# Interaction tower with table look-ups: inner pair products in two 64-column tiles, R of the first group filled by ScalarE, and small tables looked up for groups 1 and 2 only

## What is computed

```python
e  = stack([tbl_f[ids[:, f]] for f in range(26)], axis=1)            # 512 x 26 x 32
x1 = einsum('bik,bjk,hij->bhk', e,  e, W1) + b1[None, :, None]       # 128 maps
x2 = einsum('bik,bjk,hij->bhk', x1, e, W2) + b2[None, :, None]
z  = sum(concatenate([x1, x2], axis=1), axis=-1)                     # 512 x 256
h  = relu(concatenate([z, dense_ctx], axis=1) @ W_top1 + b_top1)
h  = relu(h @ W_top2 + b_top2)
y  = h @ W_top3
```

## Time and profile before

| | us |
|---|---|
| median of 3 runs (lowest, highest) | 170.41 (170.31, 170.66) |
| the profiled execution, device time | 170.0 |
| its span, first to last instruction | 168.1 |
| TensorE matmuls busy | 137.4 (82%) |
| VectorE busy | 111.0 (66%) |
| GpSimd busy | 94.9 (56%) |
| ScalarE busy | 65.5 (39%) |

### The profile page before, as it was taken

How to read it: one execution, slowest core, us unless ns; L and a number is a source line. 1 busy time by engine, 2 the same in 40 slices (tenths; PEclk the granted TensorE clock), 3 DMA queues, 4 the chain that set the end, 5 groups by cost and what they waited for, 6 DMA issues and landing times.

```text
span 168.1 us, 3668 instructions
## 1 busy us (share of the span) xinstructions
PE 137.4 (82%) x1414; PEld 124.0 (74%) x1414; DVE 111.0 (66%) x425; ACT 65.5 (39%) x177; POOL 94.9 (56%) x100
## 2 busy tenths in 40 slices
PE   6418999200099979898899999899999979999995
PEld 6305666100099959788898899789899969999993
DVE  7899368999999919999804599980659996000000
ACT  1122888400025870350453730155281024574042
POOL 4778777787778777777777777777760000000000
PEclk9965999955559999999999999999999999999999
DMA  6994331000000312001011331010042000022000
GB/s 129 387 289 157 120 98 23 12 12 13 12 18 8 65 27 75 16 12 16 12 16 17 64 78 25 16 16 12 16 80 59 5 0 4 0 51 65 17 0 0
DMA packets 8537, 8.56 MB, mean 51 GB/s; under 512 B 3128, under 2 KB 7650, under 8 KB 8340
## 3 DMA queue, kind: packets, MB, share of 16 engines
q1 hardware_dynamic: 2668, 4.70, 8.8%
q10 hardware_dynamic: 2908, 2.12, 5.7%
q0 software_dynamic: 2944, 1.51, 5.3%
HBM read 7.28 MB, written 1.04 MB: 50 GB/s over the span
## 4 chain that ended last, share of the span: by engine, by line
PE 60%; DVE 16%; POOL 8%; ACT 6%; DMA 4%; issue 4%; ACTq 0%; DVEq 0%; SPq 0%
PE ring L619 15%; PE z2p L655 14%; POOL emb L317 8%; PE z2p L660 7%; PE ring L625 5%; PE h2y L711 4%; PE ring L639 4%; DVE l L507 3%; DMA emb<-in_tbl,idx 3%; DVE r L499 3%; DVE emb L478 3%; PE ring L648 2%; PE h1p L702 2%; ACT v_in L791 2%; DVE ctx_x L474 2%
## 5 line engine op out<-in xcount | busy, mean ns | idle before, releaser
L317 POOL DMA_INDIRECT emb<-in_tbl,idx x92 | 94.0, 1022 | 29.4 <-issue 27.7
L619 PE MATMUL ring<-r,l 128*128 128x104 f32 x256 | 32.7, 287 | 15.2 <-DVE l L507 15.2
L619 PEld LDWEIGHTS ring<-r,l 128*128 128x128 f32 x256 | 31.9, 203 | 16.3 <-DVE l L507 15.4
L803 ACT COPY t_in<-ring 128x416 f32<-128x416 f32 x32 | 16.2, 506 | 34.2 <-PE ring L619 34.2
L655 PE MATMUL z2p<-t_in,v_in 128*128 128x128 f32 x208 | 24.4, 277 | 0.8 <-ACT v_in L791 0.8
L655 PEld LDWEIGHTS z2p<-t_in,v_in 128*128 128x128 f32 x208 | 23.6, 192 | 1.2 <-ACT v_in L791 1.0
L590 PE MATMUL ring<-w1s,w2t 128*128 128x352 f32 x52 | 17.2, 494 | 4.0 <-DVE w1s L371 4.0
L590 PEld LDWEIGHTS ring<-w1s,w2t 128*128 128x128 f32 x52 | 10.6, 206 | 10.1 <-DVE w1s L371 4.1
L507 DVE TENSOR_TENSOR l<-sg_b,l 128x192 f32<-128x192 f32 (+5 forms) x72 | 15.6, 300 | 0.0
L507 DVE TENSOR_TENSOR l<-sg_a,l 128x192 f32<-128x192 f32 (+5 forms) x72 | 15.6, 298 | 0.0
L474 DVE TENSOR_TENSOR ctx_x<-ring,mask 128x512 f32<-128x512 f32 x6 | 4.1, 691 | 17.2 <-PE ring L639 17.1
(11 more groups left out here) (129 smaller groups left out, 183.3 us busy)
## 6 DMA issues: line engine op xcount, KB each, us to landing
w2t<-in_L_rec_W SPq DMA_DIRECT2D x1, 1664.0 KB, 7.2
emb<-in_tbl,idx POOLq DMA_INDIRECT x92, 2.4
wt<-in_W_top SPq DMA_DIRECT2D x2, 512.0 KB, 8.4
octet<-in_octet_ids SPq DMA_DIRECT2D x1, 750.0 KB
gram_scratch<-t_in ACTq DMA_DIRECT2D x4, 169.0 KB
gram<-gram_scratch ACTq DMA_DIRECT2D x4, 126.0 KB
small_tbl<-in_tbl SPq DMA_DIRECT2D x4, 125.0 KB
w<-in_L_rec_W SPq DMA_DIRECT2D x1, 338.0 KB, 7.7
```

The costliest lines, as they stand in the source:

```text
L317: pool.indirect_dma_start(out=emb[:, g, f * K:(f + 1) * K], out_offset=None, in_=a[f"tbl_{f}"][:, :], in_offset=bass.IndirectOffsetOnAxis( ...
L619: last = pe.matmul(ps[:, i * 4 * NF:(i + 1) * 4 * NF], l[:, t, 0:P], R[:, t, :, :].rearrange("p q f -> p (q f)"), start=True, stop=True)
L803: act.copy(t_in[:, :, n * 4 * BLK:(n + 1) * 4 * BLK], ps[:, 0:BLK * 4 * NF].rearrange("p (x j) -> p j x", j=NF)).then_inc(t_out, 1)
```

## The change

1. An inner tile is computed by two matmuls with 64 stationary columns each, written to partitions 0 to 63 and 64 to 127, in place of one with 128. Both move the same 104 columns.
2. For group 0 ScalarE fills `R`, out of the single columns of `l` in SBUF. For the other groups VectorE still fills it, but later: part 0 after the inner products of the first half, part 2 after the inner products of the second.
3. The copy of part 0 into `l` waits for the inner blocks of the group before (`TB * (g - 1) + NB`), and only the fill of `R` waits for all its blocks.
4. `look_up(1)` stands ahead of the blocks of group 0 and writes to the banks of `h1p` and `h2y` in place of the ring. Layer 1 of group 0 waits for VectorE to have read them.
5. The small tables are looked up for groups 1 and 2 only (`OH_E = 3`): `look_up(3)` and `pick(3)` go, and group 3 gathers all its 26 fields, so GpSimd issues 96 transfers. The id arrays for the look-up shrink by a third.

```diff
+OH_E = 3
...
-            return [("oh", (g - OH_G) * 2 + k) for k in range(2)] if OH_G <= g < G else []
-
-        turns += [("pre", n) for n in range(EARLY, LATE)] + picks(1)
+            return [("oh", (g - OH_G) * 2 + k) for k in range(2)] if OH_G <= g < OH_E else []
+
+        turns += [("pre", n) for n in range(EARLY, LATE)]
...
+        def pick_bank(g, n):
+
+            return [h1p, h2y][n][:, :, :].rearrange("p m b -> p (m b)") if g == 1 else bank_of("oh", n)[:, :]
...
-                    if g >= OH_G and f in OH:
+                    if OH_G <= g < OH_E and f in OH:
                         continue
...
-                if g > 0 and part < 2:
-                    dve.wait_ge(t_done, TB * g)
+                if g > 0 and part == 0:
+                    dve.wait_ge(t_done, TB * (g - 1) + NB)
                 dve.wait_ge(singles, 3 * g + part + 1)
                 dve.tensor_copy(lc(c, SGL + o, w), sgt[c][:, :, o:o + w]).then_inc(singles_out, 1)
-                if g > 0 and part == 0:
+
+            def fill_r(g, part):
+
+                if g == 0:
+                    return
...
+                if part == 0:
                     dve.wait_ge(t_done, TB * g)
                 for q in range(4):
...
-                products(0, inner + across).then_inc(pairs, 2)
+                products(0, inner).then_inc(pairs, 1)
+                fill_r(g, 0)
+                products(0, across).then_inc(pairs, 1)
 
             def build_b(g):
                 take_part(g, 1)
+                fill_r(g, 1)
                 take_part(g, 2)
                 dve.wait_ge(singles_out, 3 * g + 3)
                 squares(1)
                 products(1, inner).then_inc(pairs, 1)
+                fill_r(g, 2)
                 products(1, across).then_inc(pairs, 1)
...
-                        last = pe.matmul(ps[:, i * 4 * NF:(i + 1) * 4 * NF], l[:, t, 0:P],
-                                         R[:, t, :, :].rearrange("p q f -> p (q f)"), start=True, stop=True)
+                        fields = R[:, t, :, :].rearrange("p q f -> p (q f)")
+                        s = slice(i * 4 * NF, (i + 1) * 4 * NF)
+                        pe.matmul(ps[0:HALF, s], l[:, t, 0:HALF], fields, start=True, stop=True)
+                        last = pe.matmul(ps[HALF:P, s], l[:, t, HALF:P], fields, start=True, stop=True)
...
             for n in range(EARLY):
                 prepare(n)
+            look_up(1)
             for n in range(TB):
                 t_block(0, n, True)
             for n in range(EARLY, LATE):
                 prepare(n)
-            look_up(1)
             z_group(0, True)
+            pe.wait_ge(picked_out, len(picks(1)))
...
+            def fill_r(part):
+                f0, f1 = PARTS[part]
+                c = f0 // NH
+                o, w = f0 - c * NH, f1 - f0
+                act.wait_ge(zeroed, 1)
+                act.wait_ge(singles_out, part + 1)
+                for q in range(4):
+                    s = slice(K * q, K * (q + 1))
+                    last = act.copy(R[s, :, q, f0:f1], lc(c, SGL + o, w)[s, :, :])
+                last.then_inc(r_ready, 1)
```

More of the change, by code:

```diff
@@ L143, in build @@
         yrow = sb("yrow", [1, B])
-        octet = sb("octet", [P, len(OH), B - OH_G * P], I32)
+        octet = sb("octet", [P, len(OH), (OH_E - OH_G) * P], I32)
         onehot = octet[:, :, :].bitcast(F32)
         small_tbl = sb("small_tbl", [P, len(OH), OCT * K])
-        place_in = sb("place_in", [P, G - OH_G, len(OH)], I32)
-        place = sb("place", [P, G - OH_G, len(OH)])
-        mask = sb("mask", [P, G - OH_G, len(OH), OCT])
+        place_in = sb("place_in", [P, OH_E - OH_G, len(OH)], I32)
+        place = sb("place", [P, OH_E - OH_G, len(OH)])
+        mask = sb("mask", [P, OH_E - OH_G, len(OH), OCT])
         iota_p = sb("iota_p", [P, 1], I32)
@@ L264, in rows_of @@
         def rows_of(g, f0, f1):
-            return sum(not (g >= OH_G and f in OH) for f in range(f0, f1))
+            return sum(not (OH_G <= g < OH_E and f in OH) for f in range(f0, f1))
         def lc(c, col, n):
@@ L458, in one_hot @@
                 dve.wait_ge(octet_step, 3)
-                n = (G - OH_G) * len(OH)
+                n = (OH_E - OH_G) * len(OH)
                 dve.tensor_tensor(mask[:, :, :, :].rearrange("p g f a -> p (g f) a"),
@@ L469, in pick @@
                     dve.wait_ge(picked, n + 1)
-                    src = bank_of("oh", n)[:, :].rearrange("p (f a d) -> p f a d", f=2, a=OCT)
+                    src = pick_bank(g, n).rearrange("p (f a d) -> p f a d", f=2, a=OCT)
                     pair = mask[:, g - OH_G, 2 * k:2 * k + 2, :].unsqueeze(3).to_broadcast([P, 2, OCT, K])
@@ L545, in _ @@
             split_wt1c()
-            dve.wait_ge(zeroed, 1)
             one_hot()
@@ L634, in look_up @@
                         pe.wait_ge(small_in, 16 * len(OH))
-                    pe.wait_ge(*bank_free("oh", n))
-                    ps = bank_of("oh", n)
+                    if g > 1:
+                        pe.wait_ge(*bank_free("oh", n))
+                    ps = pick_bank(g, n)
                     for i in range(2):
@@ L796, in _ @@
             act.mul(kb[:, :], cols[:, 8:10], float(K)).then_inc(kb_ready, 1)
+            for part in range(len(PARTS)):
+                fill_r(part)
             act.wait_ge(kb_ready, 1)
@@ L899 @@
     inputs = dict(inputs)
-    by_field = _np.transpose(_np.asarray(inputs["ids"])[OH_G * P:, list(OH)])
+    by_field = _np.transpose(_np.asarray(inputs["ids"])[OH_G * P:OH_E * P, list(OH)])
     inputs["octet_ids"] = _np.broadcast_to(by_field, (OR,) + by_field.shape)
-    inputs["place_ids"] = _np.transpose(by_field.reshape(len(OH), G - OH_G, P), (2, 1, 0))
+    inputs["place_ids"] = _np.transpose(by_field.reshape(len(OH), OH_E - OH_G, P), (2, 1, 0))
     nc = _bacc.Bacc("TRN2", target_bir_lowering=False, num_devices=1)
```

## The result

The changed kernel takes 163.58 us in the median of 4 runs (163.09 to 165.5), against 170.36 for the kernel before (169.71 to 170.66): a ratio of 0.963 (95% interval 0.955 to 0.971). The profiled execution took 163.09 us with a span of 161.3.

A forecast was written before the change was run, and what follows sets the result against it. TensorE bounds the kernel (82% busy), but group 3's gathers take over: start 136.0, plus blocks 10.93 - 1.4, cold clock 1.9 and tail 16.76 give span 164.2; adding 1.9 and 0.4 makes 166.5 us, range 164.0 to 168.3.

The forecast's parts named there:

- TensorE's path: TensorE up to group 3's blocks: gains summing to 9.05 us, so free at 131.4 instead of 140.41.
- the `pick` waits: Group 1's look-ups: shorter inner blocks no longer cover `pick`; about 0.5 us turns into waits, net gain 0.9.
- the start: Start of group 0's blocks: VectorE loses copies into `R` and waits for part 2's landing; 44.2, 1.6 us earlier.
- not elsewhere after 50 us: Sign to look for: the granted clock falls in front of group 3's blocks and nowhere else after 50 us.
- The price of a couple: Inner blocks: two half-tile matmuls run side by side at 0.092 us a couple instead of 0.114, 1.4 us a group.
- The two rivals built on dearer couples: Inner blocks: couples run serially at 0.184 us, 183.6 us (chance 0.05); or a 0.124 us floor, 168.1 us (0.03).
- the one in which the tiles give nothing: Inner blocks: weight loads keep a couple at 0.114 us, TensorE stays warm, 166.0 us; chance 0.10.
- The mechanism: Group 3's blocks wait for gather 94 (128.9), then VectorE's 7.05 us; start 136.0, with TensorE idle 4.6 us.
- the smaller id arrays: Start of group 0: their saving was costed at nothing, covered by VectorE's wait for part 2's landing.
- when the gathers are done: Group 3's part 1: transfer 94 leaves at 126.6 and lands 2.3 us later, at 128.9, bounds up to 130.1.
- the clock in front of group 3: TensorE's idle time before group 3 halves its clock, costing 1.9 us, bounds 0 and 2.2.
- No cooling: Rival at group 3: the clock stays up or gathers come 1 to 2 us sooner; 164.6 us, chance 0.12.

The follow-up runs named there:

- experiment 12: The changed kernel run again unchanged, with a second profile: median 164.76 us (161.92 to 166.36), ratio 0.958.
- experiment 2: The changed kernel with whole inner tiles again, one matmul with 128 stationary columns each: median 164.95 us, ratio 0.973.
- experiment 3: The changed kernel with four gathers of group 3 left out and no look-up in their place: median 161.81 us, ratio 0.956.
- experiment 5: The changed kernel with VectorE instead of ScalarE filling `R` of group 0: median 163.64 us, ratio 0.964.
- experiment 1: The changed kernel with small tables looked up for groups 1 to 3 again, 92 gathers and large id arrays: median 164.49 us, ratio 0.966.
- experiment 7: The kernel before with only group 3's look-up dropped, so it gathers all its fields: median 166.95 us against 169.8, ratio 0.983.
- experiment 8: The changed kernel with ScalarE filling parts 1 and 2 of `R` for group 3: median 163.0 us, ratio 0.958.
- experiment 4: The changed kernel with one look-up turn for group 3 (fields 3 and 5), 94 gathers: median 163.59 us, ratio 0.961.
- experiment 6: The changed kernel with 12 added identity matmuls (24 instructions) ahead of group 3's blocks: median 164.54 us, ratio 0.970.
- experiment 10: The changed kernel with 12 added identity matmuls (24 instructions) filling the gaps ahead of `z_group(0)`: median 164.47 us, ratio 0.969.
- experiment 11: The changed kernel with one look-up turn for group 3 and filled gaps ahead of `z_group(0)`: median 161.79 us against 169.92, ratio 0.952.

## Why the prediction came out as it did

**TensorE's path was right to a tenth.** Free for group 3 at 131.46, forecast 131.4. By stage: group 0's blocks began at 43.60 (44.2 forecast); group 1's at 78.60 (83.21 - 1.6 - 1.3 - 1.45 = 78.9); the round of group 1 took 28.02 us, 0.6 less than before (0.9 forecast, the `pick` waits took a little more back); that of group 2 24.84, 3.8 less, as forecast. Misses cancel in this sum: the start gained 2.3 us and not 1.6, the way from there to group 1 gained 2.35 and not 2.75. And it holds for one execution: in experiment 12 the same kernel was free at 133.89, since the clock fell in `z_group(0)`, where the prediction had expected no fall ("not elsewhere after 50 us").

**The price of a couple was right.** 0.089 us at full clock (0.092 taken). The rule quoted from the Trainium skill (TensorE: Matmul & The Clock Gate, section "Wait — 56ns, not 53.3ns?"), about 62 ns for each matmul with hardware decoding off, would make it 0.124; it does not bind here, and no run shows which way the decoding was set. The two rivals built on dearer couples are out, and so is the one in which the tiles give nothing: taking them back costs 1.8 us (experiment 2).

**The mechanism was right.** Group 3 waits for the 94th gather, then for VectorE: 127.87 to 134.95 is 7.08 us (7.05 forecast). Experiments 3, 5 and 12 show it from both sides: fewer gathers bring the start of group 3 forward, and delays of up to 3.7 us ahead of it move it by 0.2 us or less.

**A term was put at nothing: the smaller id arrays.** The prediction said that they "fall under the same wait". They moved the wait itself: part 2 of group 0 was taken at 40.44, where 41.2 was forecast, and with the large arrays put back (experiment 1) at 41.18. That is the start's extra gain: in experiment 1 the blocks of group 0 began at 44.34, within 0.15 of the forecast.

**A term was off: when the gathers are done.** Part 1 was there at 127.8, not 128.9. The 92nd transfer left at 123.04 in place of 124.11; I had carried the pace over unchanged. The steady step is 1.25 us in both; the difference is in the longer gathers up to 60 us. It ranged further between builds: part 1 was taken between 126.82 and 128.07 us in the five profiles that show a wait in front of group 3. The smaller id arrays are part of it: with them the 92nd transfer left by 123.39 at the latest, with the large ones at 123.62 at the earliest (experiment 7). From leaving to the count the last gather of part 1 took 2.3 us as forecast, but 3.7 in experiment 8 and 4.7 in experiment 4. What sets the length of the long gathers was not tried; that they are held up by what VectorE or other transfers do at the time is an untested possibility.

**The step that failed: the clock in front of group 3.** I added 1.9 us for TensorE falling to 1.2 GHz while it waits. It stayed at 2.4 GHz there through waits of 3.49, 2.43, 2.17, 1.27 and 1.19 us in five profiles; experiment 6, with added matmuls there, settles nothing. The row that I leant on, a fall 2.54 us after the last matmul, was true of one execution; in the changed kernel's profile TensorE was idle from 32.7 us and the clock stood at 1.00 for 4.5 us more, before it fell (first window above). "No cooling" (0.12), forecast at 162.3 of span, was the case that came: with the gathers 1.1 us sooner it gives 161.2, and 161.3 was measured. The two errors, 1.1 and 1.9, make up the 2.9 us between 164.2 and 161.3. Both went the same way, which is why the measured time came out at the edge of the range.

**Still open.** Executions of the changed kernel range over 4.4 us on one chip (161.92 to 166.36). The clock in group 0 explains it only in part, since the wait absorbs up to 3.5 us, and filling the gaps changed nothing (experiment 10). Nor does a low mean clock go with a long execution there: the three of 166.0 to 166.4 us had mean granted clocks of 0.948 to 0.958, the three shorter ones 0.916 to 0.935. The whole-tile kernel ranged over 0.14 us, and experiment 11 over 0.75. The unprofiled executions leave no trace, so whether the gathers land late in the long ones is not known.

## What to carry to other kernels

When a change speeds up the engine that sets the end, add up how early it will be at each place where it takes data, and compare that with the landing times of queues that are now far off the chain: here 8.5 us of slack were gone at once, and four transfers of 1.25 us became the price at that point. Moving work from a busy engine to a paced queue pays until the two meet. The best split may lie between: with filled gaps one look-up turn beat none by the ratios (0.952 against 0.969), while two turns with filled gaps were not run. As long as an engine waits at such a meeting point, a saving in front of it is worth nothing, and a loss there costs nothing up to the length of the wait (3.5 us here), so test such edits behind it or with the queue made shorter.

## What the runs showed of the hardware

- Two float32 matmuls with 64 stationary and 104 moving columns, to partitions 0 and 64, ran side by side: 0.089 us a couple at full clock. One with 128 stationary columns took 0.114. At half clock the couple took 0.173 us (21 steps from 43.83 to 47.47).
- The clock fell in a stage that is not idle. Between the across blocks and `z_group(0)` TensorE works in short pieces with gaps of 0.4 to 0.9 us. In five of nine profiles with that stage as in the changed kernel the clock fell there, and the 26 across instructions took 4.8 to 5.8 us instead of 3.1. With the gaps filled it held in both profiles; with four of nine holding anyway, two can be chance. The windows of experiment 12 show the fall:

```profile
52.00:54.60 2.60, 1.99 (x86) 1.86 (x81) 2.56 (x24) 1.59 (x4) 2.14 (x2) 1.00 0.55 90
54.60:58.00 3.40, 2.34 (x13) 1.68 (x13) 3.33 (x20) 3.29 (x7) 2.59 (x3) 0.85 0.11 27
58.00:61.00 3.00, 2.28 (x11) 2.05 (x10) 2.76 (x4) 0.75 (x2) 2.29 (x3) 0.50 0.18 38
```

- After the pause ahead of group 0 the clock came back 3.9 us after the blocks began in the changed kernel, about 6.1 in experiment 1, and 4.34 in the kernel before. The same kernel gave 3.1 in its second profile (experiment 12); all fourteen profiles lie between 3.1 and 6.2.
- A gather's time from leaving to the count was not constant: for the last of group 3's part 1 it was 2.3 us in the changed kernel, 3.7 in experiment 8 and 4.7 in experiment 4.
